# Where a tile's second up half is multiplied: eight products from the end of one group to the end of the one before

## The chip, the cores and the metric

The kernel runs on one core of a Trainium2 chip. The metric is device time in microseconds (us), from runs of the whole program; lower is better. The core has a tensor engine (TensorE, "PE" in the profile, with its weight loads as "PEld"), a vector engine (VectorE, "DVE"), a scalar engine (ScalarE, "ACT"), a general engine (GpSimd, "POOL") and a queue engine (SyncE, "SP").

## The reference

One graph layer over 4096 nodes of 512 channels with 131072 edges, everything in float32. With `src` as the row of an edge and `dst` as its column:

```
z   = layernorm(x) * g1 + b1
q,k,v = z @ Wq + bq, z @ Wk + bk, z @ Wv + bv          # 8 heads of 64
s_e = (q[row] . k[col]) / 8 + edge_bias                 # per edge and head
att = segment_softmax(s, row) applied to v[col], summed by row
x1  = x + att @ Wo + bo
ff  = silu((layernorm(x1) * g2 + b2) @ W1 + b1) @ W2 + b2   # 512 -> 1024 -> 512
out = layernorm(x + x1 + ff)
```

## The kernel before, in words

A first phase sorts the edges by row into records, computes q, k and v and writes k and v as rows to memory. The second phase, from about 1478 us of the span on, goes over 32 tiles of 128 rows, taken in order of their number of edges. For each row of a tile the kernel walks its edges in groups of 8; a tile needs 4 to 7 groups. The first four groups of a tile are unrolled and called stage 0 to stage 3 (`body(t, stage)`); the rest run in a loop with stage 4 (`further`).

The engines each run their own program over the same groups and meet at semaphores. For one group:

- GpSimd issues 8 indirect gathers (L535), one per edge slot, each with a k and v row per partition, into one of three buffers.
- VectorE multiplies q into the 8 k rows (`products`, L1021, four instructions, one per pair of slots), weights the middle two pairs of v rows of the previous group (`weigh`, L1032), rescales the running output (`scale`, L1040) and the running weights, and then takes the softmax of the group (`softmax`, L1067, L1069, L1071).
- TensorE sums the products over columns by accumulated transposes (`sum_d`, L1358, 16 instructions for each half of the group), adds the transposed weighted v rows of the group before (`turn_sum`, L1386), folds the scores (`turn_scores`, L1366), and accumulates the previous group's weighted v rows, again by transposes, pair by pair (`sum_v`, L1376).
- ScalarE copies the scores (`take_scT`, L703), weights the last pair of the previous group with 16 activations (`weigh(3)`, L731), takes the exponents (L714, L715), weights pair 0 (`weigh(0)`, L731) and copies the summed v rows in between (L709).

Instructions of one engine run in the order in which they are written. That order is fixed by hand: ScalarE's `weigh(3)` stands behind `take_scT` of the same group, and TensorE's `sum_v(3)` waits for `weigh(3)`.

The rest of the layer for a finished tile is spread over the stages of the next two tiles. While tile t runs, tile t-2 (register `older`) gets its feed-forward part: its normalized rows are transposed in stage 0 (`turn_z2`, L1407 and L741), then multiplied with W1 (`up`, L1417). The 8 blocks of 128 hidden columns are cut in two halves `a` = 0 and 1 of 4 blocks, each with 4 products over the 512 inputs, so `up(k, a, first, end)` does products `first` to `end` of 16. When all 16 are issued it tells ScalarE through H_DONE. Half 0 accumulates in one PSUM bank and half 1 in another. ScalarE's `hidden(k, a)` (8 activations, L753 and L754) reads a half: half 0 at the end of its stage 0, half 1 at the end of its stage 1, followed by the copy of the transposed attention rows (`turn_att`, L736; L1393 on TensorE). VectorE's `silu(k, a)` (L1079) waits for it in stage 1 (half 0) and in stage 2 (half 1). In stage 2 VectorE loads the next tile's group count (`count_after`, L247) between this multiply and the softmax. The products with W2 (`down`, `down_side`, L1429 and L1439) and with Wo (L1401) follow in stages 2 and 3.

Each float32 product of `up` appears in the trace as two matmul instructions of 128x128; a transpose is one.

Of the kernel before, what the change touches and what calls it, by code (L numbers as in the profile page):

```python
# [37 lines left out]
def layer_kernel(nc, x, src, dst, edge_bias, Wq, bq, Wk, bk, Wv, bv, Wo, bo, ln1_g, ln1_b,  # L38
# [37 lines left out]
    with ExitStack() as ctx:  # L76
# [172 lines left out]
        def count_after(eng, t):  # L249

            return load_count(eng, eng.snap(nc.s_assert_within(t + 1, 1, NT, skip_runtime_bounds_check_because="t is a tile")))
# [989 lines left out]
        def _(pe):  # L1241
# [99 lines left out]
            groups, now, ahead, count, coming, older = (pe.alloc_register(f"pe_{n}") for n in ("groups", "now", "ahead", "count", "coming", "older"))  # L1341
# [9 lines left out]
            def sum_d(a):  # L1351

                if a == 0:
                    pe.wait_ge(S["scT_sb_ready"], groups)
                    pe.wait_ge(S["sc_ready"], groups)
                pe.wait_ge(PRODS[a], now)
                for i in range(D // FOLD):
                    last = pe.matmul(scT_ps[:, a * P:(a + 1) * P], prod_cols[:, i, a * SH:(a + 1) * SH], ident[:, :],  # L1358
                                     start=i == 0, stop=i == D // FOLD - 1, is_transpose=True)
                if a == 1:  # L1360
                    last.then_inc(S["scT_ready"], 1)

            def turn_scores():
                pe.wait_ge(S["scT_sb_ready"], now)
                for a in range(2):
                    last = pe.matmul(sc_ps[:, a * SH:(a + 1) * SH], scT_sb[:, a * P:(a + 1) * P], fold[:, :], start=True, stop=True)  # L1366
                last.then_inc(S["sc_summed"], 1)

            def sum_v(pair):

                if pair == 0:
                    pe.wait_ge(S["vT_sb_ready"], groups)
                pe.wait_ge(V_READY[pair], ahead)
                for s in (2 * pair, 2 * pair + 1):
                    for c in range(KT):
                        last = pe.matmul(vT_ps[:, c * P:(c + 1) * P], vw[:, s, c * P:(c + 1) * P], ident[:, :],  # L1376
                                         start=s == 0 and c == 0, stop=s == GROUP - 1, is_transpose=True,
                                         skip_group_check=True)
                last.then_inc(SUMMED[pair], 1)

            def turn_sum(first=False):

                pe.wait_ge(S["vT_sb_ready"], groups)
                pe.wait_ge(S["acc_taken"], groups)
                for c in range(KT):
                    last = pe.matmul(acc_ps[:, c * P:(c + 1) * P], vT_sb[:, c * P:(c + 1) * P], ident[:, :],  # L1386
                                     start=first and c == 0, stop=c == KT - 1, is_transpose=True, skip_group_check=True)
                last.then_inc(S["acc_ready"], 1)

            def turn_att(k):  # L1390
                pe.wait_ge(S["att_ready"], k)
                for c in range(KT):
                    last = pe.transpose(turn_ps[:, c * P:(c + 1) * P], att[:, c * P:(c + 1) * P], ident[:, :])  # L1393
                last.then_inc(S["att_turned"], 1)

            def out_proj(k):

                pe.wait_ge(S["weights2"], 48)
                pe.wait_ge(S["att_sb"], k)
                for c in range(KT):  # L1400
                    last = pe.matmul(wo_ps[:, :], attT[:, c * P:(c + 1) * P], Wo_sb[:, c, :], start=c == 0, stop=c == KT - 1)  # L1401
                last.then_inc(S["wo_done"], 1)

            def turn_z2(k):
                pe.wait_ge(S["z2_ready"], k)
                for c in range(KT):
                    last = pe.transpose(turn_ps[:, c * P:(c + 1) * P], z2n[:, c * P:(c + 1) * P], ident[:, :])  # L1407
                last.then_inc(S["z2_turned"], 1)

            def up(k, a, first=0, end=HT // 2 * KT):  # L1410

                if a == 0 and first == 0:
                    pe.wait_ge(S["z2_sb"], k)
                    pe.wait_ge(S["y_taken"], k)
                for n in range(first, end):
                    m, c = a * HT // 2 + n // KT, n % KT
                    last = pe.matmul(h_ps[m // 4][:, (m % 4) * P:(m % 4 + 1) * P], W1_sb[:, c, m * P:(m + 1) * P],  # L1417
                                     z2T[:, c * P:(c + 1) * P], start=c == 0, stop=c == KT - 1, skip_group_check=True)
                if end == HT // 2 * KT:
                    last.then_inc(H_DONE[a], 1)  # L1420

            def down(k, first, end):

                if first == 0:
                    pe.wait_ge(H_READY[0], k)
                for m in range(first, end):
                    if m == HT // 2:
                        pe.wait_ge(H_READY[1], k)
                    last = pe.matmul(y_ps[:, :], hT[:, m * P:(m + 1) * P], W2_sb[:, m, :], start=m == 0, stop=m == HT - 1,  # L1429
                                     skip_group_check=True)  # L1430
                if end == HT:
                    last.then_inc(S["y_done"], 1)

            def down_side(k, m, side):

                if m == 0 and side == 0:
                    pe.wait_ge(H_READY[0], k)
                of = slice(side * C // 2, (side + 1) * C // 2)
                pe.matmul(y_ps[:, of], hT[:, m * P:(m + 1) * P], W2_sb[:, m, of], start=m == 0 and side == 0, stop=False,  # L1439
                          skip_group_check=True)  # L1440

            def body(t, stage):
                if stage == 0:
                    with pe.If(t > 1):
                        pe.reg_add(older, older, 1)
                        turn_z2(pe.snap(older))
                    pe.nop()
                sum_d(0)
                if stage < 2:
                    with pe.If(t > 0):  # L1450
                        turn_sum()
                else:
                    turn_sum(stage == 2)
                sum_d(1)
                if 0 < stage < STAGES:
                    with pe.If(t > 1):
                        if stage == 1:
                            up(pe.snap(older), 1, 0, 2)
                        else:
                            down_side(pe.snap(older), 2 * stage - 4, 0)  # L1460
                    pe.nop()
                turn_scores()
                if stage == 0:
                    with pe.If(t > 0):
                        sum_v(0)
                        sum_v(1)
                        sum_v(2)
                        with pe.If(t > 1):
                            up(pe.snap(older), 0, 0, 2)
                        sum_v(3)  # L1470
                    pe.nop()
                else:
                    sum_v(0)
                    sum_v(1)
                    if stage == 2:
                        pe.reg_mov(coming, count_after(pe, t))
                    sum_v(2)
                    if stage < STAGES:
                        with pe.If(t > 1):
                            if stage == 1:  # L1480
                                up(pe.snap(older), 1, 2, 4)
                            else:
                                down_side(pe.snap(older), 2 * stage - 4, 1)
                        pe.nop()
                    sum_v(3)
                if stage == 0:
                    with pe.If(t > 1):
                        up(pe.snap(older), 0, 2)
                if stage == 1:
                    with pe.If(t > 1):  # L1490
                        up(pe.snap(older), 1, 4)
                    with pe.If(t > 0):
                        turn_att(t)
                if stage == 2:
                    with pe.If(t > 0):
                        out_proj(t)
                    with pe.If(t > 1):
                        down(pe.snap(older), 1, 2)
                if stage == 3:
                    with pe.If(t > 1):  # L1500
                        down(pe.snap(older), 3, HT)
                for r in (groups, now, ahead):
                    pe.reg_add(r, r, 1)
# [46 lines left out]
```

## Time and profile before

| | us |
|---|---|
| median of 3 runs | 3540.56 |
| lowest and highest run | 3540.1, 3542.22 |
| the profiled execution | 3543.97 |
| its span, first to last instruction | 3542.2 |

Engine shares of the span: TensorE 80%, weight loads 61%, VectorE 75%, ScalarE 48%, GpSimd 67%. All durations below are of the one profiled execution. In a timeline a row gives start, duration, engine, line, operation, tiles, shapes and how many instructions were merged; in square brackets stands the idle time of the engine before it and what ended it. Matmul ends are modelled, so the starts of TensorE's rows are the firmer numbers. The granted clock is a share of TensorE's full 2.4 GHz; its other level is 0.5, 1.2 GHz.

### The profile page before, as it was taken

To read this page: it belongs to the slowest core of one execution; us is meant where nothing else is said; L and a number is where in the kernel's file an instruction comes from. 1 tells how busy PE (TensorE), PEld (TensorE's weight loads), DVE (VectorE), ACT (ScalarE), POOL (GpSimd) and SP (SyncE) were. 2 spreads that over 40 slices of the span, in tenths; PEclk is the share of its full clock that TensorE was granted. 3 is DMA by queue.
4 is the path that set the end of the run, shared out by engine and by line. 5 is a ranking of instruction groups with operands and counts; after the bars stand their busy time and mean duration, and the time that the engine had idled before them with its cause. 6 is when DMAs were issued, how large, how long until landed. Compare 5 with 4: busy or idle time off the path is not lost.

```text
span 3542.2 us, 83824 instructions
## 1 busy us (share of the span) xinstructions
PE 2820.5 (80%) x18957; PEld 2167.9 (61%) x18958; DVE 2646.8 (75%) x6486; ACT 1707.7 (48%) x6613; POOL 2359.2 (67%) x2567
## 2 busy tenths in 40 slices
PE   8666666666666666378999999999999999999997
PEld 7433333333333333277778878887878778787885
DVE  9776767677767667377778878778788778778875
ACT  0111111111111111177777777777877777777774
POOL 0477777777777777677766666666666666666660
PEclk9877766667777676699999999999999999999999
DMA  7322332332222322578788888888787878878660
GB/s 296 82 80 80 84 87 76 83 76 76 80 80 84 86 77 80 215 284 319 263 304 304 292 300 308 297 295 306 253 315 274 314 286 290 300 273 316 241 238 25
DMA packets 287973, 719.27 MB, mean 203 GB/s; under 512 B 89203, under 2 KB 105779, under 8 KB 287686
## 3 DMA queue, kind: packets, MB, share of 16 engines
q0 software_dynamic: 214080, 585.55, 47.4%
q1 hardware_dynamic: 73862, 133.41, 12.0%
q14 instruction: 23, 0.19, 0.0%
q8 instruction: 8, 0.13, 0.0%
HBM read 725.41 MB, written 72.97 MB: 225 GB/s over the span
## 4 chain that ended last, share of the span: by engine, by line
DVE 29%; issue 20%; POOL 18%; PE 12%; DVEq 8%; DMA 7%; ACT 3%; ACTq 1%; POOLq 1%; SPq 0%; PEld 0%; PEldq 0%
POOL records L411 17%; DVE region_c L1021 9%; DMA records<-region_c,pos_i 6%; PE bank L1358 5%; DVE region_c L1032 4%; ACT region_c L731 3%; PE bank L1258 2%; PE wide L1417 2%; DVEq L1046 2%; DVE wide L1040 1%; DVE region_c L969 1%; DVE root_t L1108 1%; PE wide L1376 1%; DMA region_a<-kv,cols 1%; DVE region_c L1079 1%
## 5 line engine op out<-in xcount | busy, mean ns | idle before, releaser
L535 POOL DMA_INDIRECT region_a<-kv,cols x1176 | 1172.5, 997 | 507.2 <-issue 430.2
L411 POOL DMA_INDIRECT records<-region_c,pos_i x1024 | 1011.6, 988 | 445.8 <-issue 411.9
L731 ACT ACTIVATE region_c<-region_a,pr 128x64 f32 x4704 | 1171.3, 337 | 33.7 <-issue 33.7
L1021 DVE TENSOR_TENSOR region_c<-region_a,bank 128x1024 f32<-128x1024 f32 x588 | 679.5, 1216 | 70.9 <-issue 47.8
L1358 PE MATMUL bank<-ident,region_c 128*128 128x128 f32 x4704 | 610.2, 285 | 148.7 <-DVE region_c L1021 144.8
L1358 PEld LDWEIGHTS bank<-ident,region_c 128*128 128x128 f32 x4704 | 578.9, 196 | 185.4 <-issue 175.3
L1376 PE MATMUL wide<-ident,region_c 128*128 128x128 f32 x4704 | 576.6, 276 | 26.6 <-ACT region_c L731 14.6
L1376 PEld LDWEIGHTS wide<-ident,region_c 128*128 128x128 f32 x4704 | 523.5, 144 | 68.2 <-ACT region_c L731 68.2
L653 ACT COPY region_c<-region_a 128x64 f32 x128 | 32.5, 254 | 1065.0 <-DMA records<-region_c,pos_i 1065.0
L1316 PE MATMUL bank<-region_b,region_a 128*128 128x512 f32 x768 | 489.3, 796 | 0.0
L1032 DVE TENSOR_TENSOR region_c<-region_a,bank 128x1024 f32<-128x1024 f32 x294 | 344.8, 1215 | 0.5 <-issue 0.5
L1316 PEld LDWEIGHTS bank<-region_b,region_a 128*128 128x128 f32 x768 | 189.4, 259 | 252.3 <-issue 252.3
L1303 PEld LDWEIGHTS wide<-region_c 64*128 64x128 f32 x2048 | 167.0, 241 | 241.2 <-issue 241.2
L933 DVE SCALAR_TENSOR_TENSOR region_c<-region_a,region_c 128x128 bf16<-128x128 int16 x1024 | 292.4, 350 | 24.0 <-issue 24.0
L1303 PE MATMUL wide<-region_c 64*128 64x64 f32 x2048 | 185.4, 334 | 154.2 <-issue 154.2
L703 ACT COPY region_c<-bank 128x256 f32<-128x256 f32 x147 | 54.7, 372 | 467.3 <-PE bank L1358 467.3
L1417 PE MATMUL wide<-region_c,region_b 128*128 128x128 f32 x2048 | 253.9, 275 | 3.2 <-ACT region_c L741 3.2
L1417 PEld LDWEIGHTS wide<-region_c,region_b 128*128 128x128 f32 x2048 | 240.9, 192 | 3.7 <-ACT region_c L741 3.7
L951 DVE TENSOR_TENSOR pos_i<-region_c 128x8 int32<-128x8 f32 x128 | 21.6, 169 | 273.8 <-DMA records<-region_c,pos_i 269.0
L1323 PE MATMUL bank<-ident,region_a 128*128 128x128 f32 x128 | 35.7, 435 | 229.4 <-DVE region_a L965 229.4
L1258 PE MATMUL bank<-region_c 128*64 128x64 bf16 x2048 | 180.4, 318 | 1.4 <-DVE region_c L852 0.6
L1429 PE MATMUL wide<-region_b,region_c 128*128 128x512 f32 x392 | 178.4, 592 | 0.0
(187 smaller groups left out, 3309.6 us busy)
## 6 DMA issues: line engine op xcount, KB each, us to landing
region_a<-srcT SPq DMA_DIRECT2D x128, 256.0 KB
region_a<-kv,cols POOLq DMA_INDIRECT x1176, 5.8
region_a<-hiT SPq DMA_DIRECT2D x256, 64.0 KB
records<-region_c,pos_i POOLq DMA_INDIRECT x1024
x_rows<-region_c SPq DMA_DIRECT2D x32, 512.0 KB, 3.4
kv<-region_a SPq DMA_DIRECT2D x32, 512.0 KB
records<-region_c SPq DMA_DIRECT2D x32, 480.0 KB, 14.8
region_a<-in_x_dram SPq DMA_DIRECT2D x32, 256.0 KB
```

Source lines behind the costliest of these rows:

```text
L411: pool.indirect_dma_start(records, bass.IndirectOffsetOnAxis(ap=pos_i[j % 2][:, s:s + 1], axis=0), rec_w[j % 2][:, s, :], None).then_inc(S ...
L535: pool.indirect_dma_start(KV[r][:, s, :], None, kv, bass.IndirectOffsetOnAxis(ap=cols[r][:, s:s + 1], axis=0), bounds_check=L - 1, oob_is_ ...
L731: last = act.activation(vw[:, s, of], v_part[:, s, C + hd * D:C + (hd + 1) * D], ACT.Copy, scale=pr[:, s + 1, hd:hd + 1])
L933: last = dve.scalar_tensor_tensor(eq[:, s * P:(s + 1) * P], srcb[b][:, s * P:(s + 1) * P], src_f[:, bass.ds(st * STREAMS + s, 1)], tri[:, ...
L1021: last = dve.tensor_tensor(prods[:, of, :], kv_in[:, of, 0:C], q_ps[:, :].unsqueeze(1).broadcast_to([P, 2, C]), ALU.mult)
L1032: dve.tensor_tensor(vw[:, s:s + 2, :].rearrange("p s (h d) -> p s h d", h=HEADS), kv_in[:, s:s + 2, C:2 * C].rearrange("p s (h d) -> p s h ...
L1258: last = pe.matmul(count_ps[side * HI:(side + 1) * HI, s * LO:(s + 1) * LO], hi_oh[b][:, :, side * SIDE + s], lo_oh[b][:, :, side * SIDE + ...
L1303: last = pe.matmul(wide_ps[b][:, side, s * LO:(s + 1) * LO], hitT[b][rows, s * P:(s + 1) * P], table_sb[rows, s * LO:(s + 1) * LO], start= ...
L1316: last = pe.matmul(qkv_ps[w][:, :], zT1[:, c * P:(c + 1) * P], Wqkv[:, w, c, :], start=False, stop=c == KT - 1)
L1358: last = pe.matmul(scT_ps[:, a * P:(a + 1) * P], prod_cols[:, i, a * SH:(a + 1) * SH], ident[:, :], start=i == 0, stop=i == D // FOLD - 1, ...
L1376: last = pe.matmul(vT_ps[:, c * P:(c + 1) * P], vw[:, s, c * P:(c + 1) * P], ident[:, :], start=s == 0 and c == 0, stop=s == GROUP - 1, is ...
L1417: last = pe.matmul(h_ps[m // 4][:, (m % 4) * P:(m % 4 + 1) * P], W1_sb[:, c, m * P:(m + 1) * P], z2T[:, c * P:(c + 1) * P], start=c == 0, ...
```

## The change

Before, half 0's products were done in stage 0 (2, then 14 at its end) and half 1's in stage 1 (2, 2, then 12 at its end). After it, half 1's first 8 products follow half 0's at the end of stage 0, and stage 1 does 2, 2 and 4. Nothing else differs: the same 32 products are issued in the same order, and the waits and signals are the same.

```diff
                     with pe.If(t > 1):
                         if stage == 1:
-                            up(pe.snap(older), 1, 0, 2)
+                            up(pe.snap(older), 1, 8, 10)
                         else:
                             down_side(pe.snap(older), 2 * stage - 4, 0)
...
                             if stage == 1:
-                                up(pe.snap(older), 1, 2, 4)
+                                up(pe.snap(older), 1, 10, 12)
...
                 if stage == 0:
                     with pe.If(t > 1):
                         up(pe.snap(older), 0, 2)
+                        up(pe.snap(older), 1, 0, 8)
                 if stage == 1:
                     with pe.If(t > 1):
-                        up(pe.snap(older), 1, 4)
+                        up(pe.snap(older), 1, 12)
```

## Rows read from the trace of the kernel before

**Rows 1.** Chain of waits, 2800 to 2868 us: its shares by line.
```profile
by line: DVE region_c L1021 24.5%; issue 16.4%; DVE region_c L1032 10.0%; DVEq L1046 3.4%; DVE root_t L1108 3.0%; DVE wide L1040 2.7%; DVE root L1110 2.2%; DVE m_run L1069 2.1%; DVE bank L1136 2.0%; DVE stats L1121 2.0%; DVE region_c L1119 
```

**Rows 2.** Chain of waits, 1990 to 2032 us: start, us, what.
```profile
2004.37 3.13 PE wide L1417 x28
2007.49 1.80 PE bank L1358 x16
...
2022.31 0.70 DVE wide L1040
```

**Rows 3.** Stretches after each tile's first product: us; PE, PEld, DVE, ACT, POOL busy; PEclk, DMA.
```profile
1641.80:1651.80 10.00, 5.68 (x39) 4.83 (x37) 7.71 (x8) 4.89 (x18) 7.71 (x10) 0.90 1.02 408
...
1990.60:2000.60 10.00, 7.16 (x47) 6.90 (x47) 8.93 (x11) 6.35 (x25) 7.09 (x8) 0.83 0.97 344
...
2807.80:2817.80 10.00, 7.58 (x66) 7.18 (x65) 8.89 (x11) 4.66 (x18) 6.19 (x7) 1.00 0.92 349
...
3427.80:3437.80 10.00, 7.67 (x52) 7.27 (x51) 8.92 (x11) 3.10 (x11) 6.27 (x7) 0.83 0.91 348
```

**Rows 4.** Timeline of the tile at 1990 us: start, us, engine, line, work, count [idle before].
```profile
1990.58 4.62 DVE L1021 TENSOR_TENSOR region_c<-region_a,bank 128x1024 f32<-128x1024 f32 x4 [0.32 <-issue]
...
1999.02 0.37 ACT L703 COPY region_c<-bank 128x256 f32<-128x256 f32 x1 [3.65 <-PE bank L1358]
...
2004.20 3.29 PE L1417 MATMUL wide<-region_c,region_b 128*128 128x128 f32 x28
...
2007.33 1.97 PE L1358 MATMUL bank<-ident,region_c 128*128 128x128 f32 x16
...
2011.57 0.37 ACT L703 COPY region_c<-bank 128x256 f32<-128x256 f32 x1 [1.26 <-PE bank L1358]
...
2014.74 0.23 DVE L1071 TENSOR_TENSOR sc<-sc,m_run 128x72 f32<-128x72 f32 x1
...
2015.85 0.20 ACT L714 ACTIVATE bank<-sc 128x32 f32<-128x32 f32 x1
...
2016.75 2.84 PE L1417 MATMUL wide<-region_c,region_b 128*128 128x128 f32 x24
...
2019.43 0.60 PE L1393 MATMUL bank<-ident,region_c 128*128 128x128 f32 x4
...
2019.87 1.97 PE L1358 MATMUL bank<-ident,region_c 128*128 128x128 f32 x16
...
2022.52 0.34 ACT L754 ACTIVATE wide<-wide,b_half 128x128 f32<-128x128 f32 x1
...
2023.35 0.68 DVE L1079 SCALAR_TENSOR_TENSOR region_c<-wide,region_c 128x512 f32<-128x512 f32 x1
...
2024.11 0.37 ACT L703 COPY region_c<-bank 128x256 f32<-128x256 f32 x1 [0.73 <-PE bank L1358]
...
2025.51 0.22 DVE L1067 TENSOR_TENSOR sc<-bank,region_c 128x64 f32<-128x64 f32 x1 [1.48 <-PE bank L1366]
```

**Rows 5.** Timeline of the tile at 2807 us.
```profile
2807.83 4.62 DVE L1021 TENSOR_TENSOR region_c<-region_a,bank 128x1024 f32<-128x1024 f32 x4 [0.33 <-issue]
...
2814.65 0.37 ACT L703 COPY region_c<-bank 128x256 f32<-128x256 f32 x1 [4.73 <-PE bank L1358]
...
2824.09 2.05 PE L1358 MATMUL bank<-ident,region_c 128*128 128x128 f32 x16 [0.97 <-DVE region_c L1021]
...
2828.41 0.37 ACT L703 COPY region_c<-bank 128x256 f32<-128x256 f32 x1 [1.49 <-PE bank L1358]
...
2840.46 0.68 DVE L1079 SCALAR_TENSOR_TENSOR region_c<-wide,region_c 128x512 f32<-128x512 f32 x1
...
2840.95 0.37 ACT L703 COPY region_c<-bank 128x256 f32<-128x256 f32 x1 [0.73 <-PE bank L1358]
...
2842.58 0.23 DVE L1067 TENSOR_TENSOR sc<-bank,region_c 128x64 f32<-128x64 f32 x1 [1.44 <-PE bank L1366]
```

**Rows 6.** Busy time, stage 1 of the tile at 1990 us, columns as rows 3.
```profile
2011.50:2022.90 11.40, 11.29 (x101) 10.91 (x100) 10.02 (x15) 11.02 (x45) 8.87 (x10) 1.00 0.93 323
```

**Rows 7.** The same, stage 4 of that tile.
```profile
2044.90:2057.60 12.70, 11.69 (x82) 9.22 (x81) 9.33 (x16) 7.85 (x33) 7.19 (x9) 1.00 0.93 331
```

## The prediction

> **What bounds the kernel now.** I read the page first. The first 16 slices of part 2 prepare the tables; the attention over the edges begins near 1478 us and fills the rest. No engine is full over the span (TensorE 80%, VectorE 75%, as the table above shows), so the question is which engine ends each stage of one tile. I therefore read the chain of waits for two tiles, then their timelines, engine by engine. A tile is 4 to 7 groups of 8 edges; its first four groups are stages 0 to 3.
>
> The chain differs between two kinds of tile. From 2800 to 2868 us it holds nearly only VectorE work: VectorE is the clock of that tile [rows 1]. From 1990 to 2032 us it goes through TensorE and ScalarE [rows 2]: from the 28 up instructions at the end of stage 0 to stage 1's column sums, to ScalarE, back to the 24 up instructions at the end of stage 1, and only in stage 2 back to VectorE (L1040).
>
> The granted clock separates them. In the first 10 us of stage 0 the tile at 1990.6 has a mean clock of 0.83, the one at 2807.8 has 1.00 [rows 3]: in the first, TensorE falls from 2.4 to 1.2 GHz for a stretch, after it had been idle before the column sums. Of the 30 tiles that carry up products, 13 show a clock below 1.00 there (first 1641.8, last 3427.8). Call them slow-clock tiles. VectorE loses nearly nothing in them today: from its first product of the tile to the second silu multiply (L1079 in stage 2) it needs 2023.35 - 1990.58 = 32.77 us in the slow-clock tile and 2840.46 - 2807.83 = 32.63 us in the other [rows 4, 5]. What the low clock does is make TensorE and ScalarE late against VectorE: the score copy of stage 0 (L703) comes 1999.02 - 1990.58 = 8.44 us after the tile's first product, against 6.82 us at full clock. Those 1.62 us are about what covers today, and the change spends them again.
>
> **The change, part by part.** One product is two instructions: 14 products are 28 instructions, 12 are 24. In stage 1, 24 instructions take from 2016.75 to the start of L1393 at 2019.43, 2.68 us, so 0.112 us each [rows 4]. Eight products, 16 instructions, leave stage 1's end and come to stage 0's end: 1.79 us. The two short pieces (4 instructions each) inside stage 1 stay where they are and do other columns. No DMA, no semaphore and no other engine's instruction moves; the new call adds no wait, only register work on TensorE's queue, at 0: from L1393 to the next group's L1358 it is 2019.87 - 2019.43 = 0.44 us for four instructions, 0.11 each, though a group's end with its register work stands between [rows 4].
>
> *Taken from stage 1's end (-1.79 us on TensorE).* Stage 2's column sums start earlier relative to stage 1's last transposes. This is worth nothing by itself, since those transposes come later by the same amount, as follows.
>
> *Added at stage 0's end (+1.79 us), slow-clock tile.* TensorE is not idle between the up products and stage 1's column sums (28 instructions from 2004.20, L1358 at 2007.33). From the stage 0 score copy to those sums it is 2007.33 - 1999.02 = 8.31 us, and from them to the stage 1 copy 2011.57 - 2007.33 = 4.24 us [rows 4]. With the move: 8.31 + 1.79 + 4.24 = 14.34 us, so the stage 1 copy moves from 2011.57 to 2013.36. Behind this copy ScalarE has in order: the last pair's 16 weighings, the exponents, pair 0's 16 weighings with the vT copy in them, and the 8 activations of the second hidden half. From the copy to the end of the last tanh (2022.52 + 0.34 = 2022.86) it is 11.29 us, and ScalarE is busy 11.02 us in the 11.4 us around it [rows 4, 6], so it can't shrink. The tanh then ends at 2013.36 + 11.29 = 2024.65 and VectorE's silu (L1079), which waits for it, starts near 2024.69 instead of 2023.35: **+1.34 us**. Softmax (L1067) follows it by 2025.51 - 2023.35 = 2.16 us (2.12 in the other tile), because the load of the next tile's group count stands between them on VectorE's queue; it lands at 2026.86. The other ways into that softmax are earlier: ScalarE is done with its attention copy (L736) at 2024.11 - 0.73 = 2023.38, then at 2025.17, and copy to softmax is 2025.51 - 2024.11 = 1.40 us: 2026.57. Stage 1's own softmax can be late by at most 1.79 us (end of L1071, 2014.74 + 0.23 + 1.79 = 2016.76), before ScalarE comes to its exponents at 2015.85 + 1.79 = 2017.64, so it does not add. The TensorE chain itself cancels: +1.79 at one end, -1.79 at the other, and stage 2's sums stay near 2019.87. After stage 2 the tile's chain is VectorE's, so the 1.34 us stay to the end of the tile and are not made up.
>
> *The same, full-clock tile.* The up products end near 2823.0; the sums start at 2824.09 after 0.97 us of idle for VectorE's products [rows 5]. The new start is 2814.65 + 8.31 + 1.79 = 2824.75, 0.66 us late. The stage 1 copy comes at 2824.75 + 4.24 = 2828.99, 0.58 late; the tanh ends at 2840.28, and VectorE reaches L1079 at 2840.46. Cost 0, with some 0.14 us of cover left; the cover is gone for a tile whose stage 0 copy is more than about 6.96 us behind its first product (6.82 here). ScalarE's L736 ends at 2840.95 - 0.73 = 2840.22, then 0.58 later at 2840.80, still before the 2840.95 at which stage 2's copy runs. If the short handover costs 0.1 us more than I think, these 17 tiles pay up to 0.1 us each.
>
> **Sum.** 13 x 1.34 = 17.4 us if the same number of tiles is hit. The number is not fixed: each tile that is 1.34 us longer moves all later ones against the places where the clock falls. Of the 30 stretches, the first 13 (tiles of five or six groups) hold 9 hits, the last 17 (four groups) only 4 [rows 3]; which share the longer tiles will show, no row tells. I take 15: 15 x 1.34 = 20.1 us. The profiled execution took 3543.97 us (span 3542.2) and goes to 3564; the median of the timed runs lies 3.41 us below it, 3540.56 + 20 = 3560.6 us. Unknowns and their ends: per slow-clock tile 0 (something covers it) to 1.79 us (the whole moved block); number of such tiles from 5 to 28.
>
> The Trainium skill ("TensorE: Matmul & The Clock Gate", "What's actually happening") says that the gate's measuring runs freely and is not restarted by a kernel. No row here shows the mechanism; it agrees with a number of hits that I can only bound.
>
> **The rivals.**
> *Hidden anyway (no change).* The late silu would be covered by something I do not see, or the hits become rare. For it: VectorE already stands 1.48 us before that softmax in a slow-clock tile [rows 4]. Against it: that idle is the count load behind the silu, and it is 1.44 us in the other tile as well [rows 5]. With 0 to 5 hits: 0 to +6.7 us, 3541 to 3547.
>
> *Faster: stage 2's softmax does wait for TensorE.* The timeline puts the 1.44 and 1.48 us before L1067 down to TensorE's L1366. If so, thinning stage 1's end should bring that softmax forward. TensorE could start stage 2's sums some 1 us earlier in a full-clock tile, but ScalarE must first end L736 (2840.22), so at most 2840.95 - 2840.22 = 0.73 us a tile: 30 x 0.73 = 22 us, 3519. It decides only where the stage 1 score copy does not get later; the rows have it 0.58 later, which leaves 0.15 us at best, 17 x 0.15 = 2.6 us. Weak.
>
> *Nearly every tile pays.* If full-clock tiles lose their 0.14 us of cover, or if the longer tiles fall on the low clock again and again: 24 to 30 tiles x 1.34 = 32 to 40 us, 3573 to 3581.
>
> *The clock falls in stage 1 too.* Stage 1 keeps mostly transposes once the products leave. Had TensorE's clock fallen there, its 16 sums of 1.80 us would double as in stage 0 of slow-clock tiles, in 30 tiles at least 30 x 1.8 = 54 us: 3595. Stage 4 of the tile at 1990 holds nothing but transposes and the small fold, with a granted clock of 1.00 over 12.7 us [rows 7], which speaks against it. The Trainium skill (same page, "Part 4: PE-mode transpose") says that transposes do not count as busy for the gate in the same way and do not bring the full clock; these rows differ from it, and the rows decide.
>
> **How the numbers follow.** Forecast (6 to 23 hits, +8 to +31 us) 0.67; hidden or few hits 0.17; faster 0.06; nearly every tile 0.07; clock in stage 1 0.03. A change below 0.2% (7.1 us) is not told from none. Faster 0.06; same 0.17; slower 0.77. The range goes from 3541 (nothing shows) to 3578 (28 tiles x 1.34 = 37.5); the forecast's own range is 3549 to 3572.
>
> **What would show it.** L1417 x44 and x8 where x28 and x24 stood. In slow-clock tiles the stage 1 copy (L703) 14.34 us after the stage 0 copy instead of 12.55, then L1079 of stage 2 with an idle of about 1.3 us released by ScalarE, and 34.1 us after the tile's first product instead of 32.8. In full-clock tiles no idle before stage 1's sums, and 32.6 us as before. I am wrong if slow-clock tiles keep 32.8 us; if full-clock tiles grow as well; or if stage 2's softmax comes earlier than 34.7 us after the first product of a full-clock tile.

## The result, and the profile after

| | before | after |
|---|---|---|
| median, us | 3540.33 | 3581.00 |
| lowest to highest, us | 3538.69 to 3542.22 | 3577.91 to 3583.42 |
| profiled execution, us | 3543.97 | 3578.81 |
| its span, us | 3542.2 | 3577.0 |

The changed kernel is slower: ratio 1.011, 95% interval 1.0097 to 1.0123, 40.7 us. The forecast was 3560.6 us with a range of 3541 to 3578, so the direction was right, the size half of what came, and the range 3 us too short.

A tile whose TensorE clock falls in stage 0, in the timeline of the profiled execution after; the lines answer to those of [rows 4].

```profile
2946.64 4.61 DVE L1021 TENSOR_TENSOR region_c<-region_a,bank 128x1024 f32<-128x1024 f32 x4 [0.33 <-issue]
...
2949.14 2.81 PE L1358 MATMUL bank<-ident,region_c 128*128 128x128 f32 x16 [2.07 <-DVE region_c L1021]
...
2955.07 0.37 ACT L703 COPY region_c<-bank 128x256 f32<-128x256 f32 x1 [6.46 <-PE bank L1358]
...
2960.26 5.08 PE L1417 MATMUL wide<-region_c,region_b 128*128 128x128 f32 x44
...
2965.17 1.97 PE L1358 MATMUL bank<-ident,region_c 128*128 128x128 f32 x16
...
2969.41 0.37 ACT L703 COPY region_c<-bank 128x256 f32<-128x256 f32 x1 [3.04 <-PE bank L1358]
...
2970.63 0.22 DVE L1067 TENSOR_TENSOR sc<-bank,region_c 128x64 f32<-128x64 f32 x1 [1.05 <-PE bank L1366]
...
2974.59 1.06 PE L1417 MATMUL wide<-region_c,region_b 128*128 128x128 f32 x8
...
2980.38 0.34 ACT L754 ACTIVATE wide<-wide,b_half 128x128 f32<-128x128 f32 x1
2980.75 0.69 DVE L1079 SCALAR_TENSOR_TENSOR region_c<-wide,region_c 128x512 f32<-128x512 f32 x1 [0.81 <-ACT wide L754]
2981.10 0.39 ACT L703 COPY region_c<-bank 128x256 f32<-128x256 f32 x1
...
2982.88 0.23 DVE L1067 TENSOR_TENSOR sc<-bank,region_c 128x64 f32<-128x64 f32 x1 [1.44 <-PE bank L1366]
```

The stage 1 score copy follows the stage 0 copy by 2969.41 - 2955.07 = 14.34 us, the forecast number. VectorE now stands before L1079, and ScalarE's last tanh is what releases it; before, there was no idle on that line. L1079 comes 2980.75 - 2946.64 = 34.11 us after the tile's first product (32.77 before).

The idle before it is 0.81 us and not the forecast 1.3, because VectorE already loses the first part in stage 1. That stage's softmax (L1067) waits 1.05 us, released by TensorE, where in the tile at 1990 us it waited 0.58:

```profile
2014.08 0.22 DVE L1067 TENSOR_TENSOR sc<-bank,region_c 128x64 f32<-128x64 f32 x1 [0.58 <-issue]
```

VectorE comes out of stage 1 some 0.47 us late, and L1079 adds the rest.

A tile with the full clock, as in [rows 5]:

```profile
3176.76 4.61 DVE L1021 TENSOR_TENSOR region_c<-region_a,bank 128x1024 f32<-128x1024 f32 x4 [0.33 <-issue]
...
3183.57 0.37 ACT L703 COPY region_c<-bank 128x256 f32<-128x256 f32 x1 [5.08 <-PE bank L1358]
...
3193.67 1.96 PE L1358 MATMUL bank<-ident,region_c 128*128 128x128 f32 x16
...
3197.91 0.37 ACT L703 COPY region_c<-bank 128x256 f32<-128x256 f32 x1 [2.04 <-PE bank L1358]
...
3209.38 0.68 DVE L1079 SCALAR_TENSOR_TENSOR region_c<-wide,region_c 128x512 f32<-128x512 f32 x1
...
3211.50 0.23 DVE L1067 TENSOR_TENSOR sc<-bank,region_c 128x64 f32<-128x64 f32 x1 [1.44 <-PE bank L1366]
```

TensorE's idle before stage 1's sums is gone (0.97 us before), the copy is 0.58 us later, and L1079 comes 32.62 us after the first product, where it was 32.63: free for VectorE.

The group of L1079 over 1700 to 3450 us (busy us, mean ns | idle before it, what ended it), after and then before:

```profile
L1079 DVE SCALAR_TENSOR_TENSOR region_c<-wide,region_c 128x512 f32<-128x512 f32 x56 | 38.5, 687 | 18.6 <-ACT wide L754 18.6
```

```profile
L1079 DVE SCALAR_TENSOR_TENSOR region_c<-wide,region_c 128x512 f32<-128x512 f32 x56 | 38.3, 684 | 0.0
```

What differs from the forecast is how many tiles are hit. In the stretches of 10 us after each tile's first product (columns as in [rows 3]) 24 of 30 show a clock below 1.00, against 13 before. Twenty of them stand in one unbroken run; its first two and last two rows are shown, and the row after it:

```profile
1858.60:1868.60 10.00, 7.16 (x48) 6.88 (x47) 8.93 (x11) 6.36 (x25) 6.29 (x7) 0.83 0.82 286
1927.10:1937.10 10.00, 7.17 (x48) 6.92 (x48) 8.93 (x11) 6.40 (x25) 7.11 (x8) 0.83 0.91 313
...
3004.50:3014.50 10.00, 7.40 (x50) 7.01 (x49) 8.87 (x11) 3.02 (x11) 6.79 (x7) 0.83 0.99 374
3062.40:3072.40 10.00, 7.45 (x50) 7.05 (x49) 8.90 (x11) 3.06 (x11) 6.80 (x7) 0.83 0.98 376
...
3120.30:3130.30 10.00, 7.47 (x65) 7.07 (x64) 8.92 (x11) 4.71 (x18) 6.92 (x8) 1.00 0.98 365
```

Before, from tile 3 to tile 19, hit tiles stood alone or in pairs with a full-clock tile after them (the first tile is tile 0). The starts of the low clock's stretches show why they no longer do. Two that lie four tiles apart, from the same kernel:

```profile
1929.61:1933.02 3.41, 3.41 (x17) 3.41 (x18) 3.41 (x4) 2.24 (x8) 2.06 (x2) 0.50 0.93 356
...
2202.67:2206.08 3.41, 3.08 (x15) 3.11 (x16) 3.41 (x4) 2.62 (x10) 2.03 (x3) 0.50 0.94 317
```

They are (2202.67 - 1929.61) / 4 = 68.27 us apart per tile, and the tiles themselves are (2200.50 - 1927.06) / 4 = 68.36 us long. So the fall comes back at nearly the same place of the tile each time: 2.1 to 2.7 us after the first product in the ten hit tiles of five groups. A full-clock tile of five groups is 66.9 us long (66.8 before), and the next one finds another place. In the hit tiles of four groups the match is less close: the falls are 58.03 us apart and the tiles 57.86 us long on average, so the fall comes some 0.15 us later in each, from 2.63 us after the first product (tile 16) to 3.82 (tile 24), and tile 25 escapes.

### The profile page after: what moved, and what is told of

Its sections match the earlier page's. It is cut to its first block, busy times and chain, and to the rows that moved or that the text cites. A ratio compares the mean times of both kernels' runs of the same rounds, so it can differ in the third digit from the quotient of the medians.

```text
span 3577.0 us, 83824 instructions
## 1 busy us (share of the span) xinstructions
PE 2839.3 (79%) x18957; PEld 2183.5 (61%) x18958; DVE 2651.0 (74%) x6486; ACT 1705.5 (48%) x6613; POOL 2365.0 (66%) x2567
## 4 chain that ended last, share of the span: by engine, by line
issue 22%; POOL 20%; DVE 17%; PE 17%; ACT 8%; DMA 7%; DVEq 6%; ACTq 2%; POOLq 1%; PEld 0%; SPq 0%; PEldq 0%
POOL records L411 19%; PE bank L1358 7%; ACT region_c L731 6%; DVE region_c L1021 6%; DMA records<-region_c,pos_i 5%; PE wide L1417 4%; PE bank L1258 2%; DVE region_c L1032 1%; DVEq L1046 1%; POOL region_a L535 1%; ACTq L731 1%; PE wide L1376 1%; DVE root_t L1108 1%; DMA region_a<-kv,cols 1%; PE wide L1386 1%
## 5 line engine op out<-in xcount | busy, mean ns | idle before, releaser
L1358 PE MATMUL bank<-ident,region_c 128*128 128x128 f32 x4704 | 627.2, 290 | 138.6 <-DVE region_c L1021 135.7
L1358 PEld LDWEIGHTS bank<-ident,region_c 128*128 128x128 f32 x4704 | 594.4, 197 | 175.8 <-issue 166.1
```

## The experiments

The ratio is to the kernel before in the same session (median 3540.80 for the first four, 3543.35 for the next four, 3541.08 for the last two). "Tiles hit" are counted in the stretches of 10 us as above.

| run | median us | ratio, 95% interval | tiles hit |
|---|---|---|---|
| e1_after_again | 3580.06 | 1.0114 (1.0099 to 1.0129) | 26 |
| e2_after_filled | 3540.85 | 1.0002 (0.9993 to 1.0011) | 0 |
| e3_before_filled | 3538.30 | 0.9992 (0.9983 to 1.0001) | 0 |
| e4_four_moved | 3551.33 | 1.0032 (1.0019 to 1.0044) | 18 |
| e5_after_longer_tiles | 3600.02 | 1.0157 (1.0142 to 1.0173) | 9 |
| e6_before_count_early | 3535.18 | 0.9979 (0.9970 to 0.9988) | 9 |
| e7_after_count_early | 3542.95 | 1.0000 (0.9991 to 1.0009) | 12 |
| e8_after_filled_count_early | 3527.70 | 0.9958 (0.9944 to 0.9971) | 0 |
| e9_four_filled_count_early | 3514.38 | 0.9928 (0.9914 to 0.9941) | 0 |
| e10_before_filled_count_early | 3531.25 | 0.9972 (0.9962 to 0.9982) | 0 |

In the five filled kernels tile 2, which also waits for its data, is left out of the count; its clock there was 0.86 in e9, 0.90 in e10 and 1.00 in the others. Each count is that of one profiled execution.

### e1_after_again: the same kernel once more

> The changed kernel again, nothing edited. Theory A (the cost is paid only by tiles whose TensorE clock is at 1.2 GHz in stage 0, 1.34 us each over the same tile before, some 1.5 us over a full-clock tile; only their number was mis-sized): 3578 to 3584, with 22 to 28 of 30 tiles low, and the time goes with that number. Theory B (the longer handover also costs at full clock): the same time, but the full-clock tiles of four groups last over 56.8 us instead of 56.35.

Measured 3580.06 us with 26 tiles hit. The three full-clock tiles of four groups last 56.39 us, from first product to first product; the 13 hit ones 57.87. Theory A holds, B falls.

### e2_after_filled and e3_before_filled: the idle time filled

```diff
                         turn_z2(pe.snap(older))
+                        for i in range(16):
+                            pe.transpose(h_ps[1][:, (i % 4) * P:(i % 4 + 1) * P], ident[:, :], ident[:, :])
```

> The changed kernel, and TensorE's idle time before stage 0's column sums is filled with 16 transposes of the identity into the bank of the second up half (they are overwritten by the products). They take 1.79 us, which the 1.96 us of idle hold. Theory A: no tile loses the clock in stage 0 except perhaps tile 2, every four-group tile lasts 56.3 to 56.4 us, and the time falls from 3581 to about 3537 to 3541. Theory B: the clock is back but the time stays over 3560.

> The kernel before with the same 16 transposes. Theory A: the low clock was covered before (0.14 us a tile, 13 tiles), so it gains 0 to 2 us: 3538 to 3541. A rival (the low clock costs the kernel before as well, and the change only made that visible): a gain of over 5 us.

The changed kernel with the fill stands at 3540.85 us, level with the kernel before (ratio 1.0002). Two of its stretches, of five and of four groups:

```profile
1919.70:1929.70 10.00, 8.90 (x79) 8.50 (x78) 8.90 (x11) 7.98 (x32) 7.09 (x8) 1.00 0.88 303
...
2916.00:2926.00 10.00, 8.93 (x79) 8.53 (x78) 8.92 (x11) 4.69 (x18) 6.74 (x7) 1.00 0.98 356
```

Sixteen useless transposes a tile take back 3580.06 - 3540.85 = 39.2 us: nearly the whole loss needs the low clock. In the kernel before the same fill is worth 2.5 us, with an interval that ends at no change (0.9983 to 1.0001). The 2.6 us between the two filled kernels are within their intervals. So the low clock was covered before, and the move spent the cover. The rival of e3 falls.

### e4_four_moved: half the move

```diff
-                            up(pe.snap(older), 1, 8, 10)
+                            up(pe.snap(older), 1, 4, 6)
...
-                                up(pe.snap(older), 1, 10, 12)
+                                up(pe.snap(older), 1, 6, 8)
...
-                        up(pe.snap(older), 1, 0, 8)
+                        up(pe.snap(older), 1, 0, 4)
...
-                        up(pe.snap(older), 1, 12)
+                        up(pe.snap(older), 1, 8)
```

> Four of the 16 products of the second half are moved to stage 0's end, not eight: stage 1 does 2, 2 and 8. The moved block is 0.89 us. Theory A: a slow-clock tile's silu of stage 2 comes 8.44 + 8.31 + 0.89 + 4.24 + 11.33 = 33.21 us after its first product, 0.45 us later than before, a full-clock tile pays nothing; with 8 to 15 low tiles that is 4 to 7 us: 3544 to 3548. Theory C (the price goes with the moved work, 40.7 us for eight products): half, 3560.

Measured 3551.33, 10.5 us over the kernel before: above A's 3544 to 3548, far below C's 3560. The price of a hit tile is as said. In the timeline of the tile that starts at 2922.70:

```profile
2955.91 0.69 DVE L1079 SCALAR_TENSOR_TENSOR region_c<-wide,region_c 128x512 f32<-128x512 f32 x1 [0.36 <-ACT wide L754]
```

L1079 comes 2955.91 - 2922.70 = 33.21 us after the first product, the number expected. The miss is again the count: 18 tiles, not 8 to 15. A hit tile of four groups lasts 57.00 us against 56.33, so 18 x 0.67 = 12 us, less the 13 x 0.13 = 1.7 us that the kernel before pays: 10.4. It is a quarter of the loss for half the move, since the first 0.45 us of the moved block are covered even in a hit tile, and since 18 tiles are hit and not 24 to 26.

### e5_after_longer_tiles: is it the tile's length that makes the falls repeat?

```diff
                 dve.bn_stats(stats[:, :], z2)
                 dve.drain()
+                for i in range(2):
+                    dve.bn_stats(stats[:, :], z2)
+                    dve.drain()
...
                         down(pe.snap(older), 3, HT)
+                        for i in range(14):
+                            pe.transpose(h_ps[1][:, (i % 4) * P:(i % 4 + 1) * P], ident[:, :], ident[:, :])
```

> The changed kernel with every tile made longer without touching stages 0 to 2: in stage 3 VectorE takes the statistics of z2 three times instead of once (0.77 us each, 1.54 us more), and TensorE does 14 transposes of the identity after the last W2 product, so that its idle time before the next tile's stage 0 stays as it is. Theory A2 (24 to 26 of 30 tiles were hit because the slow-clock tile's length of 68.3 and 57.87 us comes back to the same place against the clock's stretches each time): with 1.54 us more the coincidence is gone and under 12 tiles are hit. The loop from tile 2 to 31 is 29 x 1.54 = 45 us longer by the padding and 15 to 30 us shorter by the hits that are gone: 3595 to 3612. Rival (the change itself makes TensorE's clock fall more readily): 24 or more tiles are hit again, 3625.

Measured 3600.02 us and 9 tiles hit, both as theory A2 has it. Three neighbouring stretches:

```profile
1930.60:1940.60 10.00, 7.19 (x50) 6.86 (x49) 8.91 (x11) 6.55 (x26) 7.10 (x8) 0.83 0.93 307
2000.40:2010.40 10.00, 7.16 (x62) 6.91 (x62) 8.93 (x11) 7.98 (x32) 7.09 (x8) 1.00 0.92 317
2068.70:2078.70 10.00, 7.15 (x48) 6.83 (x47) 8.88 (x11) 6.35 (x25) 7.10 (x8) 0.83 0.90 314
```

The order of the work in stages 0 to 2 is that of the changed kernel, and TensorE's idle time ahead of stage 0's sums is no shorter (2.0 to 2.4 us in tiles 16 to 31, where it was 2.0 to 2.3), yet the tiles hit fall from 24 and 26 to 9. Between the first products of tiles 2 and 31 it is 1841.16 us against 1820.46: 20.7 us more, although the padding alone adds 29 x 1.54 = 44.7. Of the difference, 24 us, 14 fewer hits among tiles 3 to 30 give 20.3 us at 1.45 us each. Tile 2, which was 4.5 us shorter than in the changed kernel with its padding left out, gives the rest. So with the order of the work and the idle time kept, the length of the tile decides how often the fall comes back. That the change makes the clock no readier to fall is not shown by this; the table under e7 shows why.

### e6_before_count_early and e7_after_count_early: what ends the idle before stage 2's softmax

```diff
                 else:
+                    if stage == 2:
+                        dve.reg_mov(coming, count_after(dve, t))
                     weigh()
                     dve.tensor_copy(sc[:, 0, :], m_run[:, :])
...
-                if stage == 2:
-                    dve.reg_mov(coming, count_after(dve, t))
                 if stage < STAGES:
```

> The kernel before, with VectorE's load of the next tile's group count (stage 2) moved from ahead of the softmax to between the products and the weighing. Theory A (the 1.44 to 1.48 us of idle before stage 2's softmax are this load on VectorE's own queue, and not the wait for TensorE that the timeline names): the softmax comes up to 0.3 to 0.4 us earlier in a full-clock tile until TensorE and ScalarE end the wait, 3528 to 3535. Rival (it is the wait for TensorE): no change, 3540.

> The changed kernel with the same edit of the count load. Theory A: slow-clock tiles gain 0.46 us each and full-clock tiles 0.59; with 17 to 25 tiles hit 3562 to 3568. Rival as before: 3581.

e6 gained 3543.35 - 3535.18 = 8.2 us; its time lies at the slow end of the expected 3528 to 3535. Its tile that starts at 2801.86, a full-clock one:

```profile
2834.48 0.68 DVE L1079 SCALAR_TENSOR_TENSOR region_c<-wide,region_c 128x512 f32<-128x512 f32 x1
2834.97 0.37 ACT L703 COPY region_c<-bank 128x256 f32<-128x256 f32 x1 [0.73 <-PE bank L1358]
2836.19 0.23 DVE L1067 TENSOR_TENSOR sc<-bank,region_c 128x64 f32<-128x64 f32 x1 [1.03 <-PE bank L1366]
```

The softmax comes 2836.19 - 2801.86 = 34.33 us after the first product instead of 34.75 [rows 5], and now the named releaser is the true one: copy to softmax is 1.22 us, where it was 1.63. Before the edit the load of the count was the later of the two, as the chain of waits said and the timeline's releaser did not. Full-clock tiles of four groups get 0.34 us shorter (56.00 from 56.34), those of five groups 0.24; hit tiles of five groups stay at 66.97 us.

e7 came out at 3542.95 us, some 20 us better than expected: 12 tiles were hit, not 17 to 25. The gain per tile was as expected (of four groups, the one that was hit 57.36 us instead of 57.87, full-clock ones 55.75 instead of 56.39). The hits did not end where the tiles got shorter, though. Of the twelve tiles of five groups (3 to 14) ten are hit, as in the changed kernel; of the tiles from 16 on none is. In these, TensorE's idle time ahead of stage 0's sums is shorter. One tile each of the kernel before, of the changed kernel and of e7:

```profile
2810.33 2.04 PE L1358 MATMUL bank<-ident,region_c 128*128 128x128 f32 x16 [1.96 <-DVE region_c L1021]
```

```profile
3179.26 2.04 PE L1358 MATMUL bank<-ident,region_c 128*128 128x128 f32 x16 [2.32 <-DVE region_c L1021]
```

```profile
2928.74 2.04 PE L1358 MATMUL bank<-ident,region_c 128*128 128x128 f32 x16 [1.59 <-DVE region_c L1021]
```

In tiles 3 to 15 this idle time is 2.3 to 2.5 us in nearly every tile of every kernel without the fill. In tiles 16 to 31 it differs:

| run | tiles 3 to 15 hit, of 13 | idle ahead of the sums, tiles 16 to 31, us | of these 16 hit |
|---|---|---|---|
| before | 8 | 1.6 to 2.0 | 4 |
| after | 11 | 2.0 to 2.3 | 12 |
| e1_after_again | 12 | 2.0 to 2.3 | 13 |
| e4_four_moved | 9 | 2.0 to 2.4 | 9 |
| e5_after_longer_tiles | 7 | 2.0 to 2.4 | 1 |
| e6_before_count_early | 8 | 1.6 to 1.8 | 0 |
| e7_after_count_early | 11 | 1.6 to 1.7 | 0 |

So the move itself lengthened that idle time in the tiles of four groups. In a full-clock tile the move brings stage 2's score copy forward from 33.12 to 32.84 us after the first product, TensorE ends the tile earlier by about as much, and VectorE, which the sums wait for, does not. e5 shows that a long idle time alone does not bring the hits; e6 and e7 have both another length and a shorter idle time, and e4 has 9 hits of 16 with a length that does not repeat the fall. How much of the rise from 13 to 24 is the repeating length and how much the longer idle time was not separated.

### e8, e9 and e10: the two edits together, with eight, four and no products moved

Each is the fill and the early count, on the kernel after, on e4's and on the kernel before; no new edit.

> The changed kernel with TensorE's idle time filled by 16 transposes and the count load early. Theory A: no tile but tile 2 loses the clock, stage 2's softmax comes 0.6 to 0.7 us earlier since ScalarE's score copy is 0.28 us earlier than in the kernel before: 3520 to 3525, faster than both kernels. Rival: as e2_after_filled, 3541.

> Four products moved instead of eight, TensorE's idle time filled with 16 transposes, the count load early. Theory A: with four moved a full-clock tile's stage 1 sums start no later than before and its stage 2 score copy comes 32.26 us after the first product (e4_four_moved) instead of 32.84, so the softmax is limited by VectorE alone, at about 33.9 us instead of 34.09: 0.2 us a tile or 6 us below e8_after_filled_count_early, which stood at 3527.7 against 3543.35 for the kernel before on the same chip; a ratio of 0.993 to 0.995. Rival (eight is as good, VectorE's queue decides at 34.09): 0.996.

> No product moved, TensorE's idle time filled, the count load early. Theory A: the softmax of stage 2 waits for the score copy at 33.12 us, so it comes at 34.34 us in every tile, 0.25 us later than with eight moved: 7 us above e8_after_filled_count_early, a ratio of 0.997 to the kernel before. If it is no slower than with eight moved, the moved products have no worth of their own.

e8 lies at 3527.70 against 3543.35, 15.7 us faster than the kernel before, and its stage 2 softmax comes 34.09 us after the first product instead of 34.74; the absolute 3520 to 3525 was missed by 3 us, which is also what that session's kernel before lay above the other sessions'. e10's ratio of 0.9972 is the 0.997 expected: with nothing moved the softmax waits for the score copy at 33.1 us. The intervals of e8 and e10 overlap, so that eight moved products beat none rests on the traces: from the first product of tile 3 to that of tile 31 it is 1694.8 us in e10, 1687.9 in e8 and 1680.0 in e9. e9 is the best kernel of all, 26.7 us faster than before (0.9928), slightly better than the 0.993 to 0.995 expected. Its tile that starts at 2790.88:

```profile
2802.87 4.18 PE L1417 MATMUL wide<-region_c,region_b 128*128 128x128 f32 x36
...
2807.14 2.05 PE L1358 MATMUL bank<-ident,region_c 128*128 128x128 f32 x16
...
2811.46 0.37 ACT L703 COPY region_c<-bank 128x256 f32<-128x256 f32 x1 [1.49 <-PE bank L1358]
...
2823.15 0.39 ACT L703 COPY region_c<-bank 128x256 f32<-128x256 f32 x1
2823.50 0.68 DVE L1079 SCALAR_TENSOR_TENSOR region_c<-wide,region_c 128x512 f32<-128x512 f32 x1
2824.78 0.23 DVE L1067 TENSOR_TENSOR sc<-bank,region_c 128x64 f32<-128x64 f32 x1 [0.59 <-PE bank L1366]
```

With four products moved, stage 1's sums start 16.26 us after the first product, as with none moved, so the stage 1 copy stays at 20.58; and the stage 2 copy is at 32.27, against 33.12 with none and 32.84 with eight. The softmax follows at 33.90, 1.63 us after the copy where e6 needed 1.22. Its idle of 0.59 us is about the 0.58 that stands before stage 1's softmax in a full-clock tile, with no other engine named: VectorE is again what bounds it, whatever the row names. Thinning stage 1's end is thus worth something, but only as much as fits in stage 0's idle time, with the clock up and the count load out of the way.

## Why the prediction was right or wrong

*The moved block: right.* 44 instructions from 2960.26 to the next start at 2965.17 are 4.91 us, 0.112 each; 16 are 1.79.

*The price of a slow-clock tile: right in sum.* Copy to copy 14.34 us as forecast, L1079 at 34.11 us (forecast 34.1), softmax at 2982.88 - 2946.64 = 36.24 us (forecast 2026.86 - 1990.58 = 36.28). A hit tile of four groups is 57.86 us long on average against 56.47 before, +1.39; of five groups 68.32 against 66.94, +1.38 (forecast +1.34). One step on the way was wrong: stage 1's softmax was said not to add, and VectorE loses its first 0.47 us there. The end stands because ScalarE's chain up to L1079 sets it either way, so only the forecast idle of 1.3 us was missed (0.81).

*The full-clock tile: right.* Sums at 3193.67 - 3176.76 = 16.91 us (forecast 2824.75 - 2807.83 = 16.92), copy at 21.15 (21.16), cost 0.06 us a tile. Stage 2's copy was said to stay at its place and comes 0.28 us earlier.

*The number of slow-clock tiles: wrong.* "I take 15" is the step that failed. It was 24 and 26 in the two profiled executions. I had written that a longer tile moves all later ones against the places where the clock falls, and then took a number near the old one, as if the hits fell at random. They do not. A hit makes the tile 1.4 us longer than before, and at that length the fall meets the next tile at nearly the same place; e5 shows that another length undoes it. A second step was put at nothing: thinning stage 1's end was called "worth nothing by itself", but it ends TensorE's tile some 0.3 us earlier and lengthens the idle time ahead of stage 0's sums in the tiles of four groups from 1.6-2.0 us to 2.0-2.3 us. Those 16 tiles hold 4 of the hits before and 12 and 13 after. What share each of the two has stays open. The rival that named the repeated hits ("fall on the low clock again and again", 24 to 30 tiles, 3573 to 3581) had a chance of 0.07 and is what happened.

The profiled execution adds up: between the first products of tiles 2 and 31 it is 1820.46 - 1786.00 = 34.5 us longer. The 22 hits among tiles 3 to 30 are on average 1.51 us over a full-clock tile of the kernel before, 33.2 us, less 1.4 for the 11 hits that it had there, and 0.4 us for the six full-clock tiles: 32.2. The other 2.3 us are tile 2, and they are not the change's: the same kernel run again (e1) has a tile 2 that is 2.6 us shorter, and two hits more.

*The range: too short at the top.* 28 x 1.34 = 37.5 us was its end. 1.34 us is the price over the same tile when it was hit before; a tile that is newly hit costs 0.13 us more. With the measured 1.5 us over a full-clock tile the end would have been 28 x 1.5 - 1.7 = 40.3 us.

*The rivals.* "The clock falls in stage 1" did not happen: the 16 sums of stage 1 take 1.96 to 1.97 us in both tiles shown, and no low stretch in tiles 3 to 31 starts later than 4.0 us after the first product. "Faster" is true only as a part: e6 to e10 show that stage 2's softmax has a TensorE and ScalarE limit 0.4 us ahead of the one by the count load, so the move alone could not bring it forward.

Left open: the timed runs of the changed kernel lie at 3578 to 3583 us, the two profiled ones at the lower end of that, and the profiled execution of the kernel before lies 3.6 us above its median. So the traces account for 34.8 of the 40.7 us; whether more tiles were hit in the other runs, no trace tells. Not measured either: at which other lengths the falls come back in every tile, and what the changed kernel does at its own length with the idle time of the kernel before.

## What to carry to other kernels

Work moved within a chain is free only as far as the next idle time reaches, and that must be checked in the slowest kind of iteration, not in the usual one: here 13 of 30 tiles had already spent 1.6 us of cover on a low clock, and the profile showed no cost for it. Where iterations have a fixed length and the clock can fall in each, do not take the number of falls as a constant or as random: here 1.4 us more in the length went with twenty hits in a row, and another 1.5 us freed most tiles. Look also at what the change does to the idle time just ahead of the fall. Filling TensorE's idle time with useless transposes is a cheap way to ask how much of a loss is clock, and it can stay in the kernel.

## What the runs showed of the hardware

TensorE's low clock came in stretches in which 16 column sums took up to 2.8 us instead of 2.0. In tiles 3 to 31 of the seven profiled executions without the fill, each began 1.8 to 4.0 us after the tile's first product: at the end of TensorE's idle time ahead of stage 0's sums, which start at 2.5 us, or while the sums already ran. In the changed kernel their starts came back every 68.27 us through ten successive tiles of five groups (1861.34, 1929.61, ... 2475.74), and every 58.03 us through nine of four groups (2602.03, 2660.06, ... 3066.24), while the tiles were 68.2 to 68.6 and 57.8 to 58.0 us long. The Trainium skill ("TensorE: Matmul & The Clock Gate", "What's actually happening") says that the gate's measuring runs freely; these repeats agree with falls that keep to a grid of their own and not to the kernel's, and a kernel whose tiles repeat at the same distance meets them again and again.

Transposes of the identity kept the clock up: in e2, e3, e8, e9 and e10 no tile after tile 2 fell below 1.00 in the stage 0 stretches. The same page ("Part 4: PE-mode transpose") says that transposes do not count as busy for the gate in the same way. These runs differ, and the measurement decides.

A register load on an engine's own queue can hide behind the releaser that the timeline names: the 1.44 us "ended by" TensorE's L1366 were ended by the count load. With the load issued behind VectorE's products the idle time was 1.03 us, and the softmax of a full-clock tile came 0.42 us earlier.
